# Attention on one Trainium2 core: TensorE transposes the split maxima before the projection's products in step 8 of a turn

## The reference, cut to what matters

```
x = L0_attn_batch                                  # 32 x 256 tokens of 128 values, f32
x = x + 0.5 * ffn(layernorm(x), ...)               # routed experts (8 of them, 128 -> 512 -> 128)
x = x + attn(layernorm(x), W_qkv, ..., W_proj, ...)
x = x + 0.5 * ffn(layernorm(x), ...)

def attn(batch, ...):                              # b=32, n=256, 16 heads of 8 values
    qkv = sn_dense(batch, W_qkv, u_qkv, sigma_qkv)
    q, k, v = split_heads of qkv
    att = einsum('bhqd,bhkd->bhqk', q, k) * hd ** -0.5
    att = softmax(where(causal, att, big_neg))
    x = einsum('bhqk,bhkd->bhqd', att, v)          # back to (b, n, 128)
    return sn_dense(x, W_proj, u_proj, sigma_proj)
```

## Time and profile before

| | |
|---|---|
| median of 3 runs | 1154.74 us (1152.61 to 1157.74) |
| profiled execution, its own time | 1151.91 us |
| its span | 1149.8 us |
| mean granted clock of TensorE | 0.877 of full speed |
| attention, its turns | about 333 to 880 us of the span |
| in that stretch: PE, DVE, ACT, POOL busy | 490.81, 391.65, 328.24, 367.78 of 547.00 us |
| granted clock in that stretch | 0.97 |
| turn 14, from one write of `qkd` to the next | 600.26 to 615.61 us, 15.35 us, granted clock 1.00 |

### The profile page before, as it was taken

The page is one execution under the profiler, slowest core; times in us unless marked ns, Lnnn a source line. Parts: engine busy times, 40 slices in busy tenths (PEclk is TensorE's granted clock), DMA queues, the critical chain, the costliest instruction groups (busy, mean ns, idle before and its releaser), DMA issues. The chain is left out here.

```text
span 1149.8 us, 25202 instructions
## 1 busy us (share of the span) xinstructions
PE 910.6 (79%) x8020; PEld 689.5 (60%) x8054; DVE 707.3 (62%) x2090; ACT 592.5 (52%) x1538; POOL 719.7 (63%) x1170
## 2 busy tenths in 40 slices
PE   2484638999936899999999999999883455988876
PEld 1383218999933566566666666666552225977876
DVE  6587944444416677777778777778654973433332
ACT  3023506666612666666666666666562423654543
POOL 4361976444132677777777777777552596777775
PEclk9655558999968999999999999999996556999998
DMA  5370002222216555555555665555510001212121
GB/s 165 88 191 20 1 9 65 69 67 68 51 47 118 104 104 113 118 117 106 111 108 109 122 116 102 112 113 111 106 27 10 1 1 41 52 52 52 48 50 30
DMA packets 124693, 89.01 MB, mean 77 GB/s; under 512 B 13649, under 2 KB 115078, under 8 KB 124566
## 3 DMA queue, kind: packets, MB, share of 16 engines
q1 hardware_dynamic: 101782, 52.36, 20.8%
q0 software_dynamic: 8960, 18.14, 6.9%
q10 hardware_dynamic: 13824, 16.92, 6.9%
HBM read 52.23 MB, written 34.87 MB: 76 GB/s over the span
## 5 line engine op out<-in xcount | busy, mean ns | idle before, releaser
L1341 DVE TENSOR_REDUCE at_mx<-at_pp 128x2 f32<-128x512 f32 (+1 forms) x384 | 260.4, 687 | 85.9 <-PE at_pp L1199 64.7
L1131 ACT ACTIVATE at_pt<-at_pm 128x512 f32<-128x512 f32 x384 | 224.6, 597 | 143.1 <-PE at_pm L1210 92.7
L1080 POOL TENSOR_SCALAR_AFFINE_SELECT at_pt<-at_pt 128x256 f32<-128x256 f32 (+1 forms) x384 | 182.1, 485 | 127.4 <-ACT at_pt L1131 123.1
L845 ACT ACTIVATE e_ht<-e_ps_h,b1t 128x128 f32<-128x128 f32 x576 | 164.5, 371 | 119.4 <-PE e_ps_h L873 119.2
L807 POOL DMA_INDIRECT e_x<-rows,gidx x144 | 138.6, 963 | 95.0 <-DVE e_y L925 49.1
L873 PE MATMUL e_ps_h<-e_xnt,e_w1own 128*128 128x128 f32 x1152 | 157.8, 281 | 25.5 <-issue 22.0
L873 PEld LDWEIGHTS e_ps_h<-e_xnt,e_w1own 128*128 128x128 f32 x1152 | 143.9, 197 | 29.5 <-issue 28.3
L883 PE MATMUL e_ps_y<-w,e_ht 128*128 x1152 | 160.1, 283 | 0.0
L883 PEld LDWEIGHTS e_ps_y<-w,e_ht 128*128 128x128 f32 x1152 | 140.8, 193 | 1.7
L925 DVE SCALAR_TENSOR_TENSOR e_y<-e_ps_y,e_x 128x256 f32<-128x256 f32 x72 | 30.5, 424 | 143.9 <-PE e_ps_y L883 143.9
L574 POOL TENSOR_SCALAR r_atp<-r_iotab,r_colp 128x128 bf16<-128x128 bf16 x128 | 91.5, 733 | 35.9 <-DVE r_colp L712 35.9
(11 more groups left out here) (256 smaller groups left out, 1622.7 us busy)
## 6 DMA issues: line engine op xcount, KB each, us to landing
at_qkd<-at_part SPq DMA_DIRECT2D x64, 192.0 KB, 3.0
kb<-at_qkd SPq DMA_DIRECT2D x64, 96.0 KB
qs<-at_qkd ACTq DMA_DIRECT2D x64, 96.0 KB
x<-e_y SPq DMA_DIRECT2D x36, 128.0 KB, 1.8
rows<-ts_x ACTq DMA_DIRECT2D x16, 264.0 KB, 3.1
rows<-at_x SPq DMA_DIRECT2D x32, 132.0 KB
ts_x<-in_x_dram SPq DMA_DIRECT2D x16, 256.0 KB, 3.2
x_by_token<-at_xa SPq DMA_DIRECT2D x32, 128.0 KB
```

The costliest lines, as they stand in the source:

```text
L845: last = a.activation(hid_t[j % NB][:, f, :], ps_h[j % NB][:, f, :], ACT.Gelu, bias=c.b1t[:, ds(e, 1), f])
L1080: g.affine_select(out=tile, in_=tile, compare_op=ALU.is_ge, fill=0.0, base=0, pattern=[[0, n], [1, P]], channel_multiplier=-1).then_inc(ma ...
L1131: a.activation(pt[u % RING][:, :], pm[u % 2], ACT.Exp, scale=SCALE).then_inc(exped, 1)
L1341: v.tensor_reduce(out, src, axis=AX.X, op=ALU.max).then_inc(maxed, 1)
```

## The change

In PE's step 8 the transposes of the split maxima, with their three waits, are issued before the projection's two products and their wait. No instruction is added or removed, and no other stream is touched. Both parts are present in turns 1 to 30.

The diff:

```
-                    if u == 8 and has(-1):
-                        wait(pe, ont_out, b)
-                        for j in range(TPB):
-                            last = te.matmul(mi[1][:, j * D:(j + 1) * D], ont[(k - 1) % 2][:, j * P:(j + 1) * P], c.wproj[:, :],
-                                             start=True, stop=True)
-                        last.then_inc(proj_mm, 1)
                     if u == 8 and has(1):
                         wait(pe, mp_done, b + 2)
                         wait(pe, v_out, b + 4, B)
...
                         last.then_inc(mt_tr, 1)
+                    if u == 8 and has(-1):
+                        wait(pe, ont_out, b)
+                        for j in range(TPB):
+                            last = te.matmul(mi[1][:, j * D:(j + 1) * D], ont[(k - 1) % 2][:, j * P:(j + 1) * P], c.wproj[:, :],
+                                             start=True, stop=True)
+                        last.then_inc(proj_mm, 1)
```

## The result

The kernel with the new order takes 1160.76 us (median of 20 runs, 1155.12 to 1165.77), the kernel before 1155.44 us (20 runs). The ratio is 1.0044, with a 95% interval of 1.0025 to 1.0063. That is a loss of 5.3 us: under the 0.5% that the prediction took as its border of no change, but clear of noise, and 1.8 us above the top of its range.

A forecast was written before the change was run, and what follows sets the result against it. Bound: landing of new queries and keys, ACT's three reads, exponential of step 10, step 0. Terms -0.6 (turn 30), -1.1 (SP's queue), 0 for the rest make -1.7 us: median 1153.0 us, 8-in-10 range 1149 to 1159.

The forecast's parts named there:

- the chain: What sets a steady turn: queries and keys land, ACT's three reads, exponential of step 10, step 0; PE's step 8 not on it.
- 0 for the rest: In the sum, every part except turn 30 and SP's queue was put at no gain or loss.
- the prediction's own sign of being wrong: The forecast is wrong if the steady turn of 15.4 us changes by more than 0.15 us.
- Turn 30: Transposes fall into PE's wait for `ont_out`; copy and step 0 of turn 31 come earlier, a gain of 0.6 us.
- The slack of the maxima: In turn 14 the maxima's DMA was taken to land 0.58 us before step 0 starts, so its landing isn't decisive.
- The copy: ACT's copy of the maxima in step 8 starts 0.15 to 0.25 us earlier, worth nothing in steady turns.
- The projection: In PE's step 8 its products end about 0.22 us later, hidden because DVE's addition starts about 1.3 us after them.
- PE's stretch: PE's own work in step 8, 0.84 us in the old order, changes by nothing, between -0.1 and +0.1 us.
- SP's queue: Reads into `kb` behind the maxima's issue start up to 0.25 us earlier in nine turns: gain 1.1 us, bounds 0 to 2.25.
- Rival A: The maxima's landing is last in all 30 turns: gain at most 9.2 us, 1145.5 us, or 1149.6 if weaker; chance 0.12.
- Rival B: `mp_done` comes late, with the projection queued behind it: slower, 1162 us with POOL 0.6 us late; chance 0.06.
- Rival C: PE's step 8 gets 0.1 us a turn longer and nothing hides it: 3 us less 0.6, 1157.1 us; chance 0.07.

The follow-up runs named there:

- b_hold_main: The kernel before, but SP issues the maxima only when PE's scores by key of step 9 are done: 1160.11 us, ratio 1.0030 (1.0006 to 1.0055).
- the held kernels: Kernels with the maxima held back, by SP's issue (old order 1.0030, new 1.0058) or ACT's copy (new order 1.0033, 1.0070; with PE's wait moved 1.0047).
- b_mp_first: The kernel before, old order of work, but PE waits for the split maxima and their buffer ahead of the projection: 1156.21 us, ratio 0.9988.
- the padded pairs: Both orders with 32 or 64 extra products ahead of the attention: ratios to the kernel before 1.0004 and 0.9986 (old), 1.0038 and 1.0031 (new).

## Why the prediction was wrong

**The step that failed** is the line on the chain: "new queries and keys land, ACT issues three reads, exponential of step 10, step 0", with nothing of PE's step 8 on it, and then "0 for the rest" in the sum. The chain was right for the ordinary turn, and the prediction's own sign of being wrong, a change of that turn by 0.15 us, did not show: it is 15.35 us in both kernels. Its first link was taken as fixed. In the trace before, two of its turns had a landing of over 5 us, and I took the ordinary turn for all of them. What hangs on it is 2.3 us for each late landing, with the granted clock that falls behind more than half of them, and the new order makes 2.7 to 3.9 more of them. No term of the sum, and none of the rivals, was about that.

**Turn 30.** 0.6 us were predicted. From the exponential of step 8 to step 0 of turn 31 it was 3.97 us; after, it is 3.33 us, 863.71 to 867.04: a gain of 0.64. From the issue to the first product it is 2.46 us, as against 2.44, so this turn still waits for the maxima, though the profile names ACT for the product. Kernel after, timeline:

```profile
863.71 0.59 ACT L1131 ACTIVATE at_pt<-at_pm 128x512 f32<-128x512 f32 x1
...
864.19 0.37 ACT L1168 ACTIVATE at_mt<-at_mi 48x256 bf16<-48x256 bf16 x1
...
864.58 0.78 SPq L1045 DMA_DIRECT2D qs<-at_mt  x1
...
867.04 0.39 PE L1210 MATMUL at_pm<-qs,kb 128*128 128x256 bf16 x2 [0.91 <-ACT at_pt L1131]
```

**The slack of the maxima** was put at 0.58 us, from the 2.44 us between issue and use in turn 30. That turn has no reads beside it. In the five turns of `b_hold_main` in which the maxima landed last they took 3.02 to 3.86 us, so the slack was smaller than that, and a hold of 0.3 us used it up in some turns. The change moved the maxima the other way, so this did no harm here.

**The copy** came 0.26 us earlier in turn 14, at the upper bound of 0.25: ACT starts it 0.11 us before the end of the exponential. **The projection** moved by 0.31 us against the exponential's start, 0.22 predicted, and DVE's addition did not notice (1.79 us behind that start before, 1.80 after). **PE's stretch** changed by 0.02 us, within the 0.1 allowed.

**SP's queue** was priced at 1.1 us. It can't be told from nothing. In the kernels of the new order without a hold or a moved wait the turns without a late landing take 15.56 us, in those of the old order without a hold 15.61: 0.05 us less with a standard error of 0.04, or 1.5 us over 30 turns. PE's wait for the reads of `kb` went from 6.4 us to 4.0.

**Rival A**, that the waits' list is right, is refuted by the kernel after itself: the maxima are issued 0.27 us earlier in turn 14, the turn did not get shorter, and step 0 stands 0.71 us behind the exponential in every turn from 1 to 28 of both profiles. Where the maxima do land last, in the held kernels, that distance grows. **Rival B** named the right sign for the wrong reason: `b_mp_first` is at 0.9988 (0.9963 to 1.0013). **Rival C** is refuted by the 0.02 us.

**What stays open** is how PE's order reaches the landings. The fetches of PE's instructions start earlier against the writes in the new order (29 of 102 in the first band of the table; 1 of 52 in the old), which fits a stream that runs ahead sooner; no run shows why it does. In the second band, too, a larger part of the landings is late in the new order (15 of 35, 3 of 24), so the start of the fetch doesn't say all. Neither the place of the waits nor the issue of the maxima explains it by itself. That a fetch in the first band makes its landing late rests on 30 of 30 cases, and on the padded pairs, in which the late landings moved with the fetches. The Trainium skill has two sentences on it. DMA: Bandwidth & Descriptors, section Queues, rings and completion order, says that the increment of a DMA's semaphore lands only after every earlier write of that DMA engine, across its queues; landings that come 1.2 to 1.8 us later when a packet of 0.93 us slips in ahead agree with it in kind, but are longer than the packet, and no run shows on which DMA engine it went. Runtime: NRT & Kernel Launch, section Instruction fetch mechanics, says that the cost of crossing a boundary of 16 KiB in the instructions is mostly hidden. Here it is not, where the fetch falls on a landing that a whole turn waits for: the measured 2.3 us decide.

## What to carry to other kernels

Before a small shift in an order is called free, look at the slowest of the repeated turns, not only at the ordinary one: the two landings over 5 us in 29 were the term that moved. Price a stall with what follows it: where the granted clock fell, a landing 1.7 us late made its turn 3.1 us longer. A wait that holds two semaphores is named by the profile as it happens to find it; a distance that stays constant from turn to turn (0.71 us here) tells which of the two is real. And a ratio of 1.001 with an interval of half a per cent is worth a second run before a theory is built on it.

## What the runs showed of the hardware

A fetch of 16 KB of TensorE's instructions, 0.9 us on one DMA engine, that started 2.4 to 2.95 us behind the first of two DRAM writes of 192 KB each came with a landing 1.2 to 1.8 us late, in 30 of 30 cases. There were 34 such fetches in 28 turns of 15.6 us, and shifting TensorE's stream by 64 or 128 instructions moved them and the late landings to other turns. After TensorE had been idle for 2.50 us its granted clock fell from 1.00 to 0.50 and was back at 1.00 some 4 us later (turn 8 of the kernel after); a granted clock below 1.00 came with 49 of the 86 late landings in the 17 profiles, and in these with no other turn. Issuing the second write half a microsecond earlier, from another queue, did not bring the landing forward (3.69 us, 3.67 in the kernel before). A DMA of 24 KB took 2.44 us from issue to use with no reads beside it and 3.02 to 3.86 us beside the reads, and holding it back by 0.3 us cost 0.3%.
